# A graph network's edge phase: counts' product from behind the second product's first tile to the head of the step

## The chip, the cores and the metric

One core of one Trainium2 chip. The metric is the time of one execution on the device in microseconds (us). The kernel before took 1314.24 us, the median of three runs between 1310.16 and 1316.35.

## The reference, cut to what matters

Four graph layers with residual and layer norm, on 1250 nodes of 512 features and 21250 edges (sorted by their destination; each node has a loop). The change lies in the first layer, whose messages are worked out for each edge:

```
mish(x) = x * tanh(softplus(x))
h        = mish(concat(x[src], x[dst], edge_attr) @ W1 + b1)      # 21250 x 512
messages = mish(h @ W2 + b2)
agg      = segment_sum(messages, dst)
u        = mish(concat(x, agg) @ W3 + b3);  out = u @ W4 + b4
x        = layernorm(x + layernorm(x + out) * gamma + beta)
```

The other three layers need sums of x[src] over the edges into each node, and the numbers of such edges. The kernel gets them from one matrix of counts (how many edges lead from node n to node m), which it builds beside the messages, and multiplies by it in the later layers.

## The kernel before, in words

The kernel first makes two tables, P = x @ W1a + b1 and Q = x @ W1b, in DRAM (prepare). The edge phase then works on 42 blocks of 512 edges (NB = 42, four tiles of 128; the last block has fewer). Its five engine programs (edges_sync, edges_gpsimd, edges_vector, edges_scalar, edges_tensor) each run a step per block, from step -3 on, in an order that is written out by hand; steps 6 to 37 are a loop of two steps. In a step s the engines work on different blocks, and are tied by semaphores alone. Each engine takes its instructions in the written order, and a wait holds all that is behind it.

GpSimd gathers the rows of P and, added to them, of Q for the edges of a block (L228), and adds the block's window of counts (L681) and of message sums (L692) to DRAM. These go through its own queue. SyncE loads edge features.

TensorE in step s, before the change (L1066 to L1074):

- first(s+1, f) for four f, called the turns of rows below: four transposes of gathered rows (L1021), and two products with the edge features on top (L1026), to the four banks of ps_x1. The first of them waits for the gather and for VectorE's h1_of(s); the last lets ScalarE start its sigmoid for block s+1 (pre_ready).
- second(s, c) for four tiles c: h @ W2 as three products in parts, over four slices, so 12 matmuls of 512 columns (L1062). They go by turns to two banks, ps_x2[0] and ps_x2[1]. Tile 0 waits for lo_ready; tile c waits until the tile two before it is evacuated.
- adjacency(s), counts' product, between tile 0 and tile 1: a matmul of 427 columns in float16 for each tile of edges (L1035), of two one-hots, to its own bank ps_adj. It waits for the one-hots of block s (key_ready) and for the evacuation of block s-1's counts by ScalarE (adj_evac).
- sums(s-2), the window sums: eight matmuls (L1046) of one-hots with the messages' parts m_hi and m_lo, to ps_agg. They wait for the second half of message_low(s-2), among others.

VectorE in step s (L820 to L844): low(s) (L753), messages(s-2) (L771), message_high(s-2) (L780), the split of edge features for block s+3 (L736, L738), one-hots (count_one_hots L796, L797 for block s+1, one_hots L807 for s-1), x2_of(s,0) (L762, it evacuates tile 0), window_sums(s-3) (L818), more one-hots, message_low(s-2) half 0 (L787), x2_of(s,1), h1_of(s+1) in two halves (L746), x2_of(s,2), message_low(s-2) half 1 (L787), x2_of(s,3).

ScalarE in step s: sigmoid and arctangent of block s-1's second activation (L943, which waits for x2_of(s-1,3), and L948), sigmoid and arctangent of block s+1's first (L919, L924), the evacuation of counts (L912), sine of block s+1 in halves (L930), sine of s-1 (L953), and the high parts of h (L936). Two loads of an activation table lie between.

The last block has its own order, the drain: second(last,0), adjacency(last), second(last,1), sums and so on (L1087). After it come the node part of the first layer and three graph layers. Blocks that don't exist are left out, so that in step 0 there is no sums, and in step -1 only the turns of block 0.

Of the kernel before, what the change touches and what calls it, by code (L numbers as in the profile page):

```python
# [549 lines left out]
def edge_phase(nc, sb, pb, sem, edge_sem, sems_to_clear, ident, half_pi, relT, srcT, qT, idx_all, base_f, base_i, npass, iota_src,  # L550
# [11 lines left out]
    with ExitStack() as ctx:  # L562
# [446 lines left out]
        def edges_tensor(pe):  # L1009
            t = nc.tensor  # L1010

            def first(b, f):

                if b.real():
                    if f == 0:
                        pe.wait_ge(q_in[b.slot], b.slot_count(16 * TE))
                    if f % 2 == 0 and b.at(-1).real():
                        pe.wait_ge(h1_ready, b.at(-1).count(2, f // 2 + 1))
                    out = ps_x1[:, f * BE:(f + 1) * BE]
                    for c in range(TE):  # L1020
                        t.matmul(out[:, c * P:(c + 1) * P], G[:, b.slot, c * D + f * P:c * D + (f + 1) * P], ident[:, :],  # L1021
                                 start=(c == 0), stop=False, is_transpose=True)
                    if f == 0:
                        pe.wait_ge(ea_ready, b.count(1))
                    for i, w in enumerate((wc_hi, wc_lo)):
                        last = t.matmul(out, w[:, f * P:(f + 1) * P], ea_parts[:, b.slot, :], start=False, stop=(i == 1))  # L1026
                    last.then_inc(pre_ready, 1)

            def adjacency(b):
                if b.real():  # L1030
                    pe.wait_ge(key_ready, b.count(TE))
                    if b.at(-1).real():
                        pe.wait_ge(adj_evac, b.at(-1).count(1))
                    for k in range(b.tiles()):
                        last = t.matmul(ps_adj[:, 0:NC], oh_win[:, b.slot, k, :], oh_src[:, b.slot, k, :], start=(k == 0), stop=(k == b.tiles() - 1))  # L1035
                    last.then_inc(adj_ready, 1)

            def sums(b):
                if b.real():
                    pe.wait_ge(oh_ready, b.count(TE))  # L1040
                    pe.wait_ge(mlo_ready, b.count(2))
                    if b.at(-1).real():
                        pe.wait_ge(agg_evac, b.at(-1).count(1))
                    for k in range(b.tiles()):
                        for i, m in enumerate((m_hi, m_lo)):
                            last = t.matmul(ps_agg[:, :], oh_winr[:, b.slot, k, :], m[:, cols(k)], start=(k == 0 and i == 0),  # L1046
                                            stop=(k == b.tiles() - 1 and i == 1))
                    last.then_inc(agg_ready, 1)

            def second(b, c):  # L1050

                if b.real() and c < b.tiles():
                    if c == 0:
                        pe.wait_ge(lo_ready, b.count(2))
                    if c >= 2:
                        pe.wait_ge(x2_evac, b.count(TE, c - 1))
                    elif b.at(-1).real():
                        pe.wait_ge(x2_evac, b.at(-1).count(TE, c + 3))
                    for k in range(KD):
                        e = slice(k * BE + c * P, k * BE + (c + 1) * P)  # L1060
                        for i, (h, w) in enumerate(((hT_hi, w2_hi), (hT_hi, w2_lo), (hT_lo, w2_hi))):
                            last = t.matmul(ps_x2[c % 2][:, :], h[:, b.slot, e], w[:, k, :], start=(k == 0 and i == 0),  # L1062
                                            stop=(k == KD - 1 and i == 2))
                    last.then_inc(x2_ready, 1 if c + 1 < b.tiles() else TE - c)

            def step(s):  # L1066
                for f in range(KD):
                    first(s.at(1), f)
                second(s, 0)
                adjacency(s)  # L1070
                second(s, 1)
                second(s, 2)
                second(s, 3)
                sums(s.at(-2))  # L1074

            def one_pass(p):
                def node_part(r):
                    u, c0 = r // KD, r % KD * D
                    pe.wait_ge(xT_in[r], p * 32 + 32)
                    pe.sem_inc(turn, 1)  # L1080
                    for k in range(KD):
                        c = slice(c0 + k * P, c0 + (k + 1) * P)
                        for i, (h, w) in enumerate(((hT_hi, w3_hi), (hT_hi, w3_lo), (hT_lo, w3_hi))):
                            last_one = t.matmul(ps_z[r], h[:, u, c], w[:, k, :], start=(k == 0 and i == 0), stop=(k == KD - 1 and i == 2))
                    last_one.then_inc(zx_out, 1)

                def drain(last, b2nd, b3rd, b4th):  # L1087
                    second(last, 0)
                    adjacency(last)
                    second(last, 1)  # L1090
                    sums(b3rd)
                    second(last, 2)
                    second(last, 3)
                    pe.wait_ge(h1_ready, last.count(2))
                    node_part(0)
                    sums(b2nd)
                    node_part(1)
                    node_part(2)
                    sums(last)
                    pe.wait_ge(x2_evac, last.count(TE))  # L1100
                    pe.sem_inc(turn, 1)
                    for r in range(3, ZE):
                        node_part(r)
                steps(pe, p, step, drain)
# [977 lines left out]
```

## Time and profile before

| | |
|---|---|
| median of three runs | 1314.24 us |
| the profiled execution, its span | 1317.44 us, 1315.8 us |
| TensorE busy with matmuls | 1241.0 us, 94% |
| VectorE busy | 1020.1 us, 78% |
| ScalarE busy | 851.8 us, 65% |
| GpSimd busy | 697.9 us, 53% |
| L1062, second product, 2004 matmuls | 798.4 us busy |
| L1046 in 205 to 790 us, 266 matmuls | 105.0 us busy |
| L1035 in 205 to 790 us, 136 matmuls | 30.8 us busy |
| edge steps 0 to 40 | about 118 to 833 us |

Records of TensorE overlap, since matmuls are pipelined and their ends are modelled: a matmul of 512 columns has a record of 0.39 us, and the next one starts 0.23 us after it. So its busy time is not the sum of records, and the starts are what to compare. Weight loads (PEld) have records of their own. Idle time is given in brackets behind an instruction with what ended it; "issue" is time in which the engine waited for nothing that the profile shows.

### The profile page before, as it was taken

What the parts mean: (1) busy time and instruction counts of PE and PEld (TensorE: products, weight loads), DVE (VectorE), ACT (ScalarE), POOL (GpSimd) and SP (SyncE); (2) the same over time, 40 slices, a digit from 0 to 9 for tenths busy, and PEclk for the clock granted to TensorE, in tenths of its full rate; (3) what the DMA queues carried; (4) which work ended last, traced back from release to release, by engine and by line L of the source; (5) the groups of instructions that cost most, each with busy time, mean ns of one, the idle gap of its engine ahead of it and who ended that gap; (6) DMA issues with size and microseconds to landing.
All of it is one profiled execution on the core that took longest, in us unless ns stands there. A gap on an engine that the chain in (4) does not pass through costs nothing. (4 is left out here: it accounts for less than half of the span.)

```text
span 1315.8 us, 18959 instructions
## 1 busy us (share of the span) xinstructions
PE 1241.0 (94%) x5844; PEld 993.9 (76%) x5844; DVE 1020.1 (78%) x1799; ACT 851.8 (65%) x772; POOL 697.9 (53%) x482
## 2 busy tenths in 40 slices
PE   6976999999999999999999999978799987999998
PEld 5764777877777777877777777767587776888886
DVE  3425799999999999999999999866775247757444
ACT  2305999999999999999999999848523101212210
POOL 0036888888888888888888888342410000111000
PEclk9996999999999999999999999999899997999999
DMA  9996877777777777777787777798100620000001
GB/s 279 335 333 148 169 136 148 153 155 156 154 161 157 148 142 151 154 155 153 157 161 155 147 142 148 189 340 306 61 1 0 221 65 0 17 1 2 0 25 56
DMA packets 107195, 183.59 MB, mean 140 GB/s; under 512 B 34994, under 2 KB 44512, under 8 KB 106872
## 3 DMA queue, kind: packets, MB, share of 16 engines
q0 software_dynamic: 70704, 105.14, 41.0%
q1 hardware_dynamic: 29336, 65.40, 14.6%
q10 hardware_dynamic: 7088, 12.20, 2.9%
q8 instruction: 37, 0.61, 0.2%
q14 instruction: 30, 0.25, 0.1%
HBM read 141.21 MB, written 41.30 MB: 139 GB/s over the span
## 5 line engine op out<-in xcount | busy, mean ns | idle before, releaser
L228 POOL DMA_INDIRECT w_raw<-q_dram,idx_all x172 | 363.2, 2111 | 77.3 <-issue 61.5
L1062 PE MATMUL ps_x<-wA_hi,hT_hi 128*128 128x512 f32 x668 | 270.8, 405 | 1.3 <-DVE hT_lo L753 1.3
L1062 PE MATMUL ps_x<-wA_hi,hT_lo 128*128 128x512 f32 x668 | 264.0, 395 | 0.0
L1062 PE MATMUL ps_x<-wA_lo,hT_hi 128*128 128x512 f32 x668 | 263.6, 395 | 0.0
L228 POOL DMA_INDIRECT w_raw<-p_dram,idx_all x176 | 181.4, 1031 | 114.2 <-DMA q_dram<-x 60.9
L1062 PEld LDWEIGHTS ps_x<-wA_hi,hT_hi 128*128 128x128 f32 x668 | 125.4, 188 | 34.2 <-issue 1.9
L1062 PEld LDWEIGHTS ps_x<-wA_hi,hT_lo 128*128 128x128 f32 x668 | 125.2, 187 | 30.8
L1062 PEld LDWEIGHTS ps_x<-wA_lo,hT_hi 128*128 128x128 f32 x668 | 125.2, 187 | 28.5
L762 DVE TENSOR_TENSOR x<-ps_x,b 128x512 f32<-128x512 f32 x167 | 113.8, 682 | 27.0 <-PE ps_x L1062 25.1
L1743 POOL TENSOR_TENSOR tmp_n<-X,gam 128x512 f32<-128x512 f32 x10 | 13.9, 1395 | 227.0 <-DVE t_be L1828 182.4
L1021 PE MATMUL ps_x<-ident,w_raw 128*128 128x128 f32 x672 | 103.6, 278 | 19.0 <-issue 11.4
L1021 PEld LDWEIGHTS ps_x<-ident,w_raw 128*128 128x128 f32 x672 | 85.9, 144 | 43.7 <-issue 13.0
L746 DVE TENSOR_TENSOR h<-ps_x,h 128x1024 f32<-128x1024 f32 x84 | 98.3, 1210 | 3.7 <-ACT h L930 3.7
L787 DVE TENSOR_TENSOR m_lo<-m,m_hi 128x1024 fp32r<-128x1024 f32 x82 | 99.3, 1212 | 0.0
L753 DVE TENSOR_TENSOR hT_lo<-h,hT_hi 128x1024 fp32r<-128x1024 f32 x84 | 98.7, 1217 | 0.0
L771 DVE TENSOR_TENSOR m<-x,m 128x1024 f32<-128x1024 f32 x82 | 96.5, 1218 | 0.0
L930 ACT ACTIVATE h<-h,half_pi 128x1024 f32<-128x1024 f32 x84 | 92.1, 1144 | 0.5
L919 ACT ACTIVATE h<-ps_x 128x2048 f32<-128x2048 f32 x42 | 78.5, 1868 | 10.8 <-PE ps_x L1026 10.8
L936 ACT CAST hT_hi<-h 128x1024 fp32r<-128x1024 f32 x84 | 83.4, 1038 | 0.9 <-issue 0.5
L1977 PE MATMUL ps_sum<-U_hi,adjT_rest 128*128 128x512 f32 x210 | 82.6, 394 | 0.2 <-issue 0.2
L1026 PE MATMUL ps_x<-ea_parts,wc_hi 128*128 128x512 f32 x168 | 82.6, 491 | 0.0
L1977 PE MATMUL ps_sum<-U_lo,adjT_rest 128*128 128x512 f32 x210 | 81.9, 390 | 0.0
(268 smaller groups left out, 2853.6 us busy)
## 6 DMA issues: line engine op xcount, KB each, us to landing
ea_raw<-in_eaT SPq DMA_DIRECT2D x88, 128.0 KB
adj_dram<-adj_sb POOLq DMA_DIRECT2D x42, 210.2 KB
adj_dram<-agg_sb ACTq DMA_DIRECT2D x11, 640.5 KB, 12.0
U_lo<-adj_dram SPq DMA_DIRECT2D x10, 640.0 KB, 9.2
adjT_dram<-adjT_sb SPq DMA_DIRECT2D x10, 640.0 KB, 6.3
adjT_rest<-adjT_dram SPq DMA_DIRECT2D x7, 640.0 KB, 9.8
w_raw_g<-in_w SPq DMA_DIRECT2D x4, 1024.0 KB, 7.7
agg_dram<-agg_sb POOLq DMA_DIRECT2D x42, 84.0 KB
```

What stands on the lines that cost most here:

```text
L228: g.indirect_dma_start(G[:, slot, c * D:(c + 1) * D], None, rows, bass.IndirectOffsetOnAxis(ap=idx_all[:, i:i + 1], axis=0), **op).then_in ...
L746: v.tensor_tensor(h1[:, b.slot, c], ps_x1[:, c], h1[:, b.slot, c], ALU.mult).then_inc(h1_ready, 1)
L753: v.tensor_tensor(hT_lo[:, b.slot, c], h1[:, b.slot, c], hT_hi[:, b.slot, c].bitcast(F32), ALU.subtract).then_inc(lo_ready, 1)
L762: v.tensor_tensor(x2[:, b.slot, cols(c)], ps_x2[c % 2][:, :], b2[:, :], ALU.add).then_inc(x2_evac, 1 if c + 1 < b.tiles() else TE - c)
L771: v.tensor_tensor(m2[:, b.slot, c], x2[:, b.slot, c], m2[:, b.slot, c], ALU.mult).then_inc(m2_ready, 1)
L787: v.tensor_tensor(m_lo[:, c], m2[:, b.slot, c], m_hi[:, c].bitcast(F32), ALU.subtract).then_inc(mlo_ready, 1)
L930: a.activation(h1[:, b.slot, c], h1[:, b.slot, c], ACT.Sin, scale=-2.0, bias=half_pi[:, :]).then_inc(t1_ready, 1)
L936: a.copy(hT_hi[:, b.slot, c], h1[:, b.slot, c]).then_inc(hi_ready, 1)
L1021: t.matmul(out[:, c * P:(c + 1) * P], G[:, b.slot, c * D + f * P:c * D + (f + 1) * P], ident[:, :], start=(c == 0), stop=False, is_transpo ...
L1026: last = t.matmul(out, w[:, f * P:(f + 1) * P], ea_parts[:, b.slot, :], start=False, stop=(i == 1))
L1062: last = t.matmul(ps_x2[c % 2][:, :], h[:, b.slot, e], w[:, k, :], start=(k == 0 and i == 0), stop=(k == KD - 1 and i == 2))
L1977: last = t.matmul(ps_m[n % 2][:, :], adj_tile(r, k).bitcast(dt), u[:, cols(k)].bitcast(dt), start=(k == 0 and i == 0), stop=(k == R - 1 an ...
```

## The change

The call adjacency(s) moves from behind second(s, 0) to the head of TensorE's step, in front of the turns of rows. Its body and its waits are the same, and so are all other engines' programs and the drain.

```
             def step(s):
+                adjacency(s)
                 for f in range(KD):
                     first(s.at(1), f)
                 second(s, 0)
-                adjacency(s)
                 second(s, 1)
                 second(s, 2)
                 second(s, 3)
```

## Rows read from the trace of the kernel before

**Rows 1.** Windows: stretch, then busy us (instructions) of PE, PEld, DVE, ACT, POOL; clock, DMA.
```profile
205.00:800.00 595.00, 595.00 (x2873) 471.60 (x2872) 577.76 (x989) 560.99 (x409) 511.74 (x342) 1.00 0.77 153
```

**Rows 2.** Waits, 205 to 790: engine, line, for what; total us, times, longest.
```profile
ACT L943 <- DVE x L762: 28.9, 33, 1.2
DVE x L762 <- PE ps_x L1062: 14.5, 33, 0.5
...
PEld ps_agg L1046 <- issue: 4.8, 29, 0.2
```

**Rows 3.** Timeline of TensorE, 517 to 535: start, duration, what.
```profile
517.10 0.39 PE L1046 MATMUL ps_agg<-m_hi,oh_winr 128*128 128x512 f32 x1
...
522.58 0.40 PE L1062 MATMUL ps_x<-wA_hi,hT_hi 128*128 128x512 f32 x1
...
525.38 0.91 PE L1035 MATMUL ps_adj<-oh_src,oh_win 128*128 128x427 f16 x4
...
526.36 0.39 PE L1062 MATMUL ps_x<-wA_lo,hT_hi 128*128 128x512 f32 x1
...
534.52 0.39 PE L1046 MATMUL ps_agg<-m_hi,oh_winr 128*128 128x512 f32 x1
```

**Rows 4.** Timeline of VectorE, 508 to 527.
```profile
508.66 0.68 DVE L762 TENSOR_TENSOR x<-ps_x,b 128x512 f32<-128x512 f32 x1
...
509.86 0.32 DVE L796 TENSOR_SCALAR oh_src<-iota_src,srcT 128x427 f16<-128x427 f16 x1
...
512.79 2.35 DVE L746 TENSOR_TENSOR h<-ps_x,h 128x1024 f32<-128x1024 f32 x2
...
515.65 1.21 DVE L787 TENSOR_TENSOR m_lo<-m,m_hi 128x1024 fp32r<-128x1024 f32 x1
...
526.08 0.67 DVE L762 TENSOR_TENSOR x<-ps_x,b 128x512 f32<-128x512 f32 x1
```

**Rows 5.** Timeline of TensorE's weight loads, at the sums of that step.
```profile
516.99 0.19 PEld L1046 LDWEIGHTS ps_agg<-m_hi,oh_winr 128*128 128x128 f32 x1 [0.17 <-issue]
```

**Rows 6.** Timeline of VectorE and TensorE at the sums of step 2.
```profile
166.99 1.21 DVE L787 TENSOR_TENSOR m_lo<-m,m_hi 128x1024 fp32r<-128x1024 f32 x1
...
168.34 0.47 PE L1046 MATMUL ps_agg<-m_hi,oh_winr 128*128 128x512 f32 x1 [1.02 <-DVE m_lo L787]
...
168.65 0.39 PE L1046 MATMUL ps_agg<-m_lo,oh_winr 128*128 128x512 f32 x1
```

**Rows 7.** Timeline of TensorE and VectorE in step 39.
```profile
801.50 0.40 PE L1062 MATMUL ps_x<-wA_hi,hT_hi 128*128 128x512 f32 x1
...
804.51 0.69 DVE L762 TENSOR_TENSOR x<-ps_x,b 128x512 f32<-128x512 f32 x1 [0.41 <-PE ps_x L1062]
...
806.31 0.44 DVE L796 TENSOR_SCALAR oh_src<-iota_src,srcT 128x427 f16<-128x427 f16 x1
...
811.66 1.22 DVE L787 TENSOR_TENSOR m_lo<-m,m_hi 128x1024 fp32r<-128x1024 f32 x1
```

**Rows 8.** Timeline of ScalarE, 505 to 514.
```profile
505.73 1.86 ACT L919 ACTIVATE h<-ps_x 128x2048 f32<-128x2048 f32 x1
...
511.25 2.19 ACT L930 ACTIVATE h<-h,half_pi 128x1024 f32<-128x1024 f32 x2
```

**Rows 9.** Timeline of VectorE and TensorE, steps -1 to 0.
```profile
113.06 0.24 DVE L797 TENSOR_SCALAR oh_win<-iota_src,keyT 128x128 f16<-128x128 f16 x1
...
117.76 1.12 PE L1021 MATMUL ps_x<-ident,w_raw 128*128 128x128 f32 x4 [7.63 <-DVE h L746]
...
135.98 0.69 DVE L762 TENSOR_TENSOR x<-ps_x,b 128x512 f32<-128x512 f32 x1 [2.05 <-PE ps_x L1062]
```

**Rows 10.** Timeline of TensorE at the start of the drain.
```profile
834.16 0.49 PE L1062 MATMUL ps_x<-wA_hi,hT_hi 128*128 128x512 f32 x1 [1.26 <-DVE hT_lo L753]
```

**Rows 11.** Timeline of GpSimd, a gather of P rows in either step.
```profile
509.33 0.98 POOL L228 DMA_INDIRECT w_raw<-p_dram,idx_all  x1 [0.30 <-issue]
...
805.68 0.98 POOL L228 DMA_INDIRECT w_raw<-p_dram,idx_all  x1 [0.30 <-issue]
```

More of the change, by code:

```diff
@@ L1066, in step @@
             def step(s):
+                adjacency(s)
                 for f in range(KD):
@@ L1069, in step @@
                 second(s, 0)
-                adjacency(s)
                 second(s, 1)
```

## The prediction

> **What bounds the kernel now.** I read the windows first, to see where the time is: between 205 and 800 us, 45% of the span, TensorE has a product in flight all the time at a granted clock of 1.00, while VectorE is busy 578 of 595 us and ScalarE 561 [rows 1]. This is the middle of the edge phase, one step after another. Then the waits of that stretch, to see who waits for whom: in each of its 33 full steps VectorE waits 0.44 us for the second product's last tile (14.5 / 33) and ScalarE 0.88 us for VectorE (28.9 / 33); TensorE's matmuls wait for nobody, but the weight load that opens the window sums is late by a little, 4.8 us over 29 steps [rows 2]. The timeline of TensorE gives the step as it is now: sums from 517.10 and the turns of rows with the edge part behind them, the second product's tile 0 from 522.58, counts' product at 525.38, tiles 1 to 3, and sums again at 534.52 [rows 3]. That is 17.42 us, without a gap: 5.48 sums and turns, 2.80 tile 0, and 9.14 for counts and tiles 1 to 3.
>
> So TensorE bounds the step; the question is by how much, since the change adds no work. The VectorE timeline answers it. x2_of(s,0) starts at 508.66, and from there VectorE runs without a wait to the end of the second message_low, 515.65 + 1.21 = 516.86: 8.20 us [rows 4]. The sums wait for exactly this, and their weight load starts at 516.99, 0.13 after it, instead of with the product before as the others do (idle 0.17) [rows 5]. How long the hand-over takes at the least is seen in step 2, where TensorE really stood waiting (idle 1.02): message_low ends at 166.99 + 1.21 = 168.20, and the second product of the sums starts at 168.65, which with a spacing of 0.23 is as if the first had started at 168.42, 0.22 after [rows 6]. In the steady step it starts 517.10 - 516.86 = 0.24 after. **The slack at the sums is 0.02 us.** VectorE's other tie to TensorE in this stretch is the start of x2_of(s,0), which needs tile 0. In step 39, where VectorE did wait for it (idle 0.41), it starts 804.51 - 801.50 = 3.01 us after tile 0's first matmul [rows 7]. In the steady step this would allow 522.58 + 3.01 = 525.59, and VectorE comes at 526.08 [rows 3, 4]: slack 0.49. Together 0.51 us of slack in the cycle tile 0, x2_of(s,0), message_low, sums, turns, next tile 0.
>
> **The change, part by part.** It moves four matmuls and two waits, in the 41 steps 0 to 40; the last block's product, in the drain, stays. No DMA and no instruction of another engine moves.
>
> What the product costs TensorE: from 525.38 to the second product after it, 526.36, less that one's own spacing of 0.23, is 0.75 us; its records say the same, 0.91 less the 0.16 by which matmuls of 0.39 at a spacing of 0.23 overlap [rows 3]. In its new place it stands behind the sums and before the turns, a pair of neighbours that the trace does not have. The nearest row for a disturbed start is the opening of the sums in step 2, 0.31 to the next instead of 0.23 [rows 6]: 0.08 more, or as much less if a disturbance of that size around the product goes away. So 0.67 to 0.83, and I take 0.75, since four streams of the same length are the most of it in either place. TensorE's own step then stays at 17.42.
>
> The two waits at the head: VectorE writes block s+1's one-hots before h1_of, which starts at 512.79, and ScalarE evacuates the counts of block s before its sine at 511.25; the head of the next step, behind the sums, is at about 519 [rows 3, 4, 8]. Both are over by 6 us: nothing. If that cover were gone, TensorE would stand with the turns and all of the step behind it.
>
> What is later by it: tile 0 and all of the turns end 0.75 later with respect to the sums before them. The cycle without slack is now
> 8.20 (x2_of(s,0) to message_low) + 0.22 (hand-over) + 5.48 (sums, turns) + 0.75 (counts) + 3.01 (tile 0 to x2_of) = 17.66 us.
> Before, without the 0.75, it was 16.91, under TensorE's 17.42. It is now the longer of the two by 0.24 (0.16 to 0.32 by the bounds of the counts' cost). VectorE's 16.98 us of work (17.42 - 0.44) fit; its wait divides, some 0.45 before x2_of(s,0) and 0.2 before x2_of(s,3). TensorE stands 0.24 before each sums.
>
> ScalarE's first sigmoid starts at 505.73, when ScalarE comes free [rows 8]; the turns end at 522.58 less a step of 17.42, 505.16, and 0.21 after (3.01 less tile 0's 2.80) it could start. With the turns 0.75 later, and 0.24 for the stand at the sums, it waits some 0.6 for them. Its first sine half then ends 0.21 + (511.25 + 1.1 - 505.73) = 6.83 after the turns; VectorE needs that at 3.01 + (512.79 - 508.66) = 7.14: 0.3 to spare, hidden. ScalarE's idle 0.88 covers its wait. GpSimd's first gather of P rows waits for the turns, but it comes over 2 us after them: hidden; the queues get nothing new.
>
> The start: in step 0 TensorE stands 7.63 us until 117.76, and the product can go there, its last one-hot at 113.06 [rows 9]. Tiles 1 to 3 of step 0 end 0.75 earlier, and VectorE stood waiting for the last (2.05 before 135.98) [rows 9]; ScalarE's chain and then the sums of block 0, which wait for message_low, come about 0.7 earlier. From 0 (if it is ScalarE that holds step 1) to 1.5 (if step 1 gives it once more); I take 0.7.
>
> The sum: the sums of blocks 1 to 37 have 36 spacings between them, each 0.24 longer: 8.6; with the 0.7 off at the start +7.9 us. The drain begins with a wait of 1.26 of TensorE, for hT_lo [rows 10], but this follows the last tile through VectorE and is late with it, so nothing is given back. The program's later stages are as they were. From the profiled execution, 1317.4 us with 1.6 outside the span, 1325.3; that execution was 3.2 above the median of the runs, so for the median 1314.24 + 7.9 = **1322 us**.
>
> **Rivals.**
> *The cycle keeps its slack (not slower).* Place: the start of x2_of(s,0). It decides as soon as the product at the head costs under 0.51 us, or VectorE's stretch and the hand-over shrink by 0.24. Then the step is 17.42 as before and only the start's gain is left: 1314.2 - 0.7 = 1313.5, or 1312.7 with the larger start. For it: of the 0.24 at the sums 0.22 is one reading, in step 2. Against it: the records of the four, 0.91 less an overlap of 0.16, leave no room for 0.51, and VectorE's 8.20 has no idle time in it. A smaller miss, cycle at 17.5, gives 1316.
> *VectorE meets GpSimd.* The gathers of P rows run beside the one-hots. In the steady step a one-hot of 0.32 at 509.86 lies under the gather of 509.33 unharmed; in step 39, after the same kind of wait before x2_of(s,0), one at 806.31 near the end of the gather of 805.68 takes 0.44, and the stretch to message_low's end is 811.66 + 1.22 - 804.51 = 8.37 instead of 8.20 [rows 4, 7, 11]. In the changed step x2_of(s,0) comes after such a wait each time. If it costs 0.17 each time, the cycle is 17.83, 36 x 0.41 = 14.8, less 0.7: 1328. Against it: step 3, without the wait, also varies, and GpSimd's gathers will move with VectorE.
> Were one one-hot in each step held for the whole of a gather, 0.98 [rows 11], it would be 36 x 0.98 = 35 us, 1349; the 0.12 at 806.31 speaks against it, and it has 0.01 of this rival's chance.
> That strong form is a rule of the Trainium skill, SBUF — State Buffer, "Who interferes with whom": VectorE and GpSimd take a shared port pair as an exclusive lock, and the later one is blocked for the whole of the other's instruction. The trace agrees that they meet, not on the length.
> *The change does not reach the path*: TensorE held at the head by the one-hots or the evacuation. The 6 us above speak against it; its price, were the margin gone, has no bound but the step.
>
> **How the numbers follow.** The forecast, cycle of 17.58 to 17.74: 0.60, 1319 to 1325. Contention, to 1330: 0.15. Slack kept or nearly, 1313 to 1318: 0.20, of it 0.05 clearly faster by something in the start or in TensorE's neighbours that I don't see. Held at the head or other: 0.05. What can be told from no change here is 0.5%, 6.6 us, so 1320.8 and up is slower: four in five of the forecast's share, all of the contention's, 0.6 in all with a part of the others against the runs' own scatter of 6 us; same 0.34, faster 0.06. The range takes in the forecast, most of the contention and the kept slack: 1313 to 1329.
>
> **What would show it.** Right: steps of 17.6 to 17.7 us; a gap of about 0.24 before the first product of the sums, put down to m_lo; VectorE waiting before x2_of(s,0) and less before x2_of(s,3); ScalarE's L919 waiting 0.4 to 0.6 for the turns; the counts' product still 0.9 in its records. Wrong: steps of 17.42 with no gap, or one-hots above 0.32 and steps of 17.8 or more, or waits at the counts' product.

## The result, and the profile after

The changed kernel takes 1324.81 us (median of 8 runs, 1320.07 to 1327.42) against 1313.51 us before (8 runs, 1309.68 to 1316.35): ratio 1.0092, 95% interval 1.0073 to 1.0111. It is slower by 11 us; 1322 was forecast. The profiled execution took 1326.07 us, its span is 1324.4.

The windows of the changed kernel's middle stretch look as before, which is why they don't explain it [rows 1]:

```profile
205.00:800.00 595.00, 594.73 (x2819) 464.23 (x2819) 573.95 (x979) 558.11 (x405) 512.82 (x337) 1.00 0.76 152
```

The waits of 205 to 790 us name the places (engine, line, for what; total us, times, longest). ScalarE now waits 0.63 a step for the turns (21.4 / 34) and half as long for VectorE; the sums' weight load is later than it was, 0.43 instead of 0.17 [rows 2]. VectorE waits before x2_of twice a step:

```profile
ACT h L919 <- PE ps_x L1026: 21.4, 34, 0.9
PEld ps_agg L1046 <- issue: 14.1, 33, 0.7
ACT L943 <- DVE x L762: 12.9, 33, 0.5
...
DVE x L762 <- PE ps_x L1062: 8.8, 41, 0.3
DVE x L762 <- issue: 7.6, 23, 0.3
```

The timeline of TensorE in one step answers to [rows 3]. From the last product of tile 3 at 515.97 to the sums it is 0.39 us, where 0.23 is the spacing without a wait; from the first of the sums to the second it is 0.33. Counts' product takes 519.07 - 518.33 = 0.74, and the next sums come 534.05 - 516.36 = 17.69 after these:

```profile
515.97 0.40 PE L1062 MATMUL ps_x<-wA_hi,hT_lo 128*128 128x512 f32 x1
516.36 0.50 PE L1046 MATMUL ps_agg<-m_hi,oh_winr 128*128 128x512 f32 x1
516.69 0.40 PE L1046 MATMUL ps_agg<-m_lo,oh_winr 128*128 128x512 f32 x1
...
518.33 0.91 PE L1035 MATMUL ps_adj<-oh_src,oh_win 128*128 128x427 f16 x4
519.07 0.60 PE L1021 MATMUL ps_x<-ident,w_raw 128*128 128x128 f32 x4
...
522.70 0.40 PE L1062 MATMUL ps_x<-wA_hi,hT_hi 128*128 128x512 f32 x1
...
534.05 0.50 PE L1046 MATMUL ps_agg<-m_hi,oh_winr 128*128 128x512 f32 x1
```

The timeline of VectorE in the same step [rows 4]: it stands before x2_of(s,0), which comes 525.70 - 522.70 = 3.00 after tile 0's start, and the second message_low ends at 532.71 + 1.20 = 533.91, 8.21 later and 0.14 before the sums. The profile names no engine for the 0.33 in front of x2_of(s,0). That it is a wait for tile 0 is read from the starts: in all the loop's steps x2_of(s,0) comes 3.00 after tile 0, as in step 39 before, where the wait was put down to TensorE [rows 7].

```profile
525.70 0.69 DVE L762 TENSOR_TENSOR x<-ps_x,b 128x512 f32<-128x512 f32 x1 [0.33 <-issue]
...
532.71 1.20 DVE L787 TENSOR_TENSOR m_lo<-m,m_hi 128x1024 fp32r<-128x1024 f32 x1
534.10 0.69 DVE L762 TENSOR_TENSOR x<-ps_x,b 128x512 f32<-128x512 f32 x1 [0.18 <-PE ps_x L1062]
```

The cycle is closed: 6.34 (sums, counts, turns, from 516.36 to 522.70) + 3.00 + 8.21 + 0.14 = 17.69.

Landmarks on TensorE in all the profiles (us; "first" is the first turns of rows, "turns 1" those of step 0, "sums k" the first product of block k's sums, "node" the last product with W3 of the edge phase, "L1534" the first transposes of counts; the step is the loop column / 37):

```
kernel            first  ->turns 1  ->sums 0  ->sums 1  ->sums 38  step    ->node  ->L1534  ->end
before            103.30   14.46     50.58     17.51     645.03    17.433   35.57    2.11   447.24
before, again     100.87   14.29     50.63     17.51     645.79    17.454   35.60    2.28   446.93
changed           100.08   13.53     49.10     17.67     654.83    17.698   35.58    8.47   445.14
changed, second   102.26   13.97     49.59     17.65     655.93    17.728   35.59    4.39   444.82
changed, third     99.30   13.36     49.07     17.65     656.20    17.735   35.58    3.59   445.35
changed, fourth   100.38   14.05     49.58     17.66     656.04    17.731   35.57    2.63   443.79
e2 mid            101.65   14.35     50.55     17.72     656.37    17.740   35.59    2.26   445.71
e3 head+onehots   102.35   14.20     49.46     17.51     650.56    17.583   35.59    3.08   445.25
e4 before+onehots 101.23   14.29     50.58     17.51     647.51    17.500   35.58    1.98   445.82
e5 head+mlow      101.92   14.44     49.21     17.51     645.03    17.433   35.57    3.89   444.13
e6 before+mlow    101.16   14.70     50.10     17.51     644.78    17.426   35.59    2.37   445.19
e7 start only      98.40   14.04     48.95     17.66     645.82    17.455   35.58    2.68   446.47
e8 before, half   101.84   13.92     49.66     17.38     638.19    17.248   35.59    3.19   446.83
e9 head, half     102.03   13.70     49.18     17.29     642.55    17.366   35.58    2.72   444.05
```

The loss is in one column, the loop: 9.8 to 11.2 us between the profiles of the changed kernel and the first of before (9.0 to 10.4 against the second). A start shorter by 1.0 to 1.5 us, to the sums of block 0, stands against it. From the first turns to the node part the changed kernel takes 6.9 to 9.8 us more; the medians of the runs differ by 11.3. The first profile of the changed kernel has also 8.47 us in front of the first transposes of counts, and the experiments begin with whether that belongs to the change.

### The profile page after: what moved, and what is told of

Same layout as the page of the kernel before. It is cut to its first block and busy times, and to the rows that moved or that the text cites. A ratio compares the mean times of both kernels' runs of the same rounds, so it can differ in the third digit from the quotient of the medians.

```text
span 1324.4 us, 18959 instructions
## 1 busy us (share of the span) xinstructions
PE 1249.3 (94%) x5844; PEld 994.1 (75%) x5844; DVE 1024.0 (77%) x1799; ACT 855.9 (65%) x772; POOL 709.6 (54%) x482
## 5 line engine op out<-in xcount | busy, mean ns | idle before, releaser
L228 POOL DMA_INDIRECT w_raw<-q_dram,idx_all x172 | 321.6, 1870 | 76.2 <-issue 51.5
L228 POOL DMA_INDIRECT w_raw<-p_dram,idx_all x176 | 234.5, 1332 | 112.6 <-DMA q_dram<-x 59.3
L1062 PE MATMUL ps_x<-wA_hi,hT_hi 128*128 128x512 f32 x668 | 264.3, 396 | 1.3 <-DVE hT_lo L753 1.3
L762 DVE TENSOR_TENSOR x<-ps_x,b 128x512 f32<-128x512 f32 x167 | 114.2, 684 | 27.3 <-PE ps_x L1062 17.8
L919 ACT ACTIVATE h<-ps_x 128x2048 f32<-128x2048 f32 x42 | 79.2, 1887 | 32.3 <-PE ps_x L1026 32.3
```

The lines of the kernel that those rows point to most:

```text
L228: g.indirect_dma_start(G[:, slot, c * D:(c + 1) * D], None, rows, bass.IndirectOffsetOnAxis(ap=idx_all[:, i:i + 1], axis=0), **op).then_in ...
L762: v.tensor_tensor(x2[:, b.slot, cols(c)], ps_x2[c % 2][:, :], b2[:, :], ALU.add).then_inc(x2_evac, 1 if c + 1 < b.tiles() else TE - c)
```

## The experiments

"Before" is timed beside each call; ratios are against it.

**The changed kernel again.** No edit.

> The changed kernel once more, for its profile. The cycle theory (tile 0, x2_of(s,0), message_low, sums, counts, turns; 8.20 + 0.22 + 5.48 + 0.75 + 3.01): steps of 17.7 us with the sums 0.15 late in their starts. The tail theory (the rest of the loss lies behind the edge loop: GpSimd adds its counts 1.3 us after the sums' start instead of 3.4 before it, so its last additions land late and the loads of counts and sums for the first layer wait): again 8 us or so of idle time of TensorE before the first transposes of counts (L1534), against 1.7 in the kernel before. The rival for the tail, chance of one execution: 2 us there, and a span nearer 1320. Time: 1324 to 1326 by the first, 1320 to 1322 by the rival.

Measured: 1324.86 us (6 runs), ratio 1.0101 (1.0075 to 1.0128). Steps of 17.73 us, and the tail is short, 4.39, with GpSimd adding its counts 3.3 us before the sums' start. The rival for the tail holds: the 8 us was chance of one execution. But its time, 1320 to 1322, does not hold: the 4.1 us that the tail gives back are taken up by 2.2 more before the first turns, 0.9 more in the start and 1.1 more in the loop. Its steps go by turns, 17.69 and 17.8. Where they are 17.8, an instruction of VectorE behind x2_of(s,0) is held up beside a gather of GpSimd; where they are 17.69, the one that is held up stands in front of x2_of(s,0), where VectorE waits for tile 0 anyway. VectorE and then GpSimd in the step of 476 us (records of 0.48 and 0.39 for the usual 0.25 and 0.28; the gather runs from 478.00 to 478.99). The records overlap: from the start of the 0.48 to message_low it is 0.47 where 0.36 is usual, so the delay is 0.11:

```profile
478.27 0.33 DVE L796 TENSOR_SCALAR oh_src<-iota_src,srcT 128x427 f16<-128x427 f16 x1
478.51 0.48 DVE L797 TENSOR_SCALAR oh_win<-iota_src,keyT 128x128 f16<-128x128 f16 x1
478.68 0.39 DVE L807 TENSOR_SCALAR oh_winr<-iota_src,relT 128x128 fp32r<-128x128 f16 x1
478.98 1.21 DVE L787 TENSOR_TENSOR m_lo<-m,m_hi 128x1024 fp32r<-128x1024 f32 x1
```

```profile
478.00 0.99 POOL L228 DMA_INDIRECT w_raw<-p_dram,idx_all  x1 [0.30 <-DVE agg_sb L818]
```

**Counts' product between the turns and tile 0.**

```
             def step(s):
-                adjacency(s)
                 for f in range(KD):
                     first(s.at(1), f)
+                adjacency(s)
                 second(s, 0)
```

> Counts' product between the turns and tile 0, so neither at the head nor beside the sums; it is still in front of tile 0. The cycle theory: nothing changes against the changed kernel, steps of 17.7 us, ScalarE's L919 no longer waits for the turns by more than the sums' lateness, 1322 to 1326. The neighbour theory (the product costs more, or a wait bites, because it stands between the sums and the turns): steps of 17.43 as before, 1312 to 1315.

Measured: 1323.52 us, ratio 1.0085 (1.0066 to 1.0104), steps of 17.74. The product costs the same wherever it stands in front of tile 0; it is not its neighbours and not the head. ScalarE's L919 waits for the turns once in 205 to 790 us, instead of 0.63 in each step, and the step is the same, so ScalarE's wait isn't what lengthens it. Only the start differs: 50.55 to the sums of block 0, as before, where the head has 49.1 to 49.6.

**The head, with the second half of the one-hots in front of x2_of(s,0).**

```
+                count_one_hots(s.at(1), 2)
+                one_hots(s.at(-1), 2)
+                count_one_hots(s.at(1), 3)
+                one_hots(s.at(-1), 3)
                 x2_of(s, 0)
                 window_sums(s.at(-3))
-                count_one_hots(s.at(1), 2)
-                one_hots(s.at(-1), 2)
-                count_one_hots(s.at(1), 3)
-                one_hots(s.at(-1), 3)
```

> The changed kernel with VectorE's second two pairs of one-hots (1.2 us) moved from behind x2_of(s,0) to in front of it; VectorE's work is the same. The cycle theory: the stretch from x2_of(s,0) to message_low is 7.0 instead of 8.2, the cycle 16.5 and no longer the longest, so steps of 17.43 (TensorE's own) and 9 to 10 us less in the edge loop: 1312 to 1316, or 3 to 5 us more if the tail stays late. The neighbour theory: steps of 17.7 as now, 1324. A third, VectorE meeting GpSimd: steps somewhere between, with one-hots above 0.32.

Measured: 1319.09 us (12 runs), ratio 1.0049 (1.0034 to 1.0064), steps of 17.58. That falls between, and the forecast of 17.43 was wrong. The timelines of VectorE, ScalarE and TensorE in this kernel:

```profile
482.60 0.69 DVE L762 TENSOR_TENSOR x<-ps_x,b 128x512 f32<-128x512 f32 x1 [0.30 <-PE ps_x L1062]
...
492.72 0.68 DVE L762 TENSOR_TENSOR x<-ps_x,b 128x512 f32<-128x512 f32 x1
...
495.05 0.68 DVE L762 TENSOR_TENSOR x<-ps_x,b 128x512 f32<-128x512 f32 x1
495.79 1.23 DVE L746 TENSOR_TENSOR h<-ps_x,h 128x1024 f32<-128x1024 f32 x1
...
498.66 1.22 DVE L787 TENSOR_TENSOR m_lo<-m,m_hi 128x1024 fp32r<-128x1024 f32 x1
500.18 0.69 DVE L762 TENSOR_TENSOR x<-ps_x,b 128x512 f32<-128x512 f32 x1 [0.30 <-PE ps_x L1062]
```

```profile
489.05 1.89 ACT L919 ACTIVATE h<-ps_x 128x2048 f32<-128x2048 f32 x1 [0.50 <-PE ps_x L1026]
...
494.61 1.15 ACT L930 ACTIVATE h<-h,half_pi 128x1024 f32<-128x1024 f32 x1
```

```profile
482.44 0.49 PE L1046 MATMUL ps_agg<-m_hi,oh_winr 128*128 128x512 f32 x1
...
488.77 0.40 PE L1062 MATMUL ps_x<-wA_hi,hT_hi 128*128 128x512 f32 x1
...
500.01 0.49 PE L1046 MATMUL ps_agg<-m_hi,oh_winr 128*128 128x512 f32 x1
```

x2_of(s,0) no longer waits, so the first cycle is broken. The next longest goes through ScalarE. From the sums at 482.44 to tile 0, which is where the turns end, it is 6.33 (the product at the head is in it); 0.28 later ScalarE's first sigmoid starts, which stood waiting for the turns; its chain to the end of the first half of the sine, at 494.61 + 1.15 = 495.76, takes 6.71; VectorE's h1_of starts 0.03 after, at 495.79, though x2_of(s,1) in front of it began 0.74 earlier and 0.60 is usual; message_low ends 4.09 later, at 499.88, and the sums start 0.13 after that. 6.33 + 0.28 + 6.71 + 0.03 + 4.09 + 0.13 = 17.57. In 31 of 32 steps of the loop h1_of starts 0.03 to 0.06 after the sine, and in none of the changed kernel's steps (0.16 to 0.46). There this cycle is 17.55, only 0.14 below the one through x2_of(s,0), and shortening that one alone could not bring the step below it.

The expectations that follow were written with another reading of this run: a cycle over two steps, with 17.28 for VectorE from x2_of(s,3) at 482.60 to message_low's end. It gives 17.57 too, but the 17.28 has VectorE's wait for the sine in it, 0.14 in this step. VectorE's own part is 17.14 here and 17.23 on average over the loop, since some one-hots are slower than in the kernel before, which makes that cycle 17.50 here and 17.55 on average. The two are close, and the one through ScalarE is the longer. This is read from the trace; no run tests it by itself.

**The kernel before, with the same one-hots in front.**

> The kernel before with the same move of one-hots on VectorE. The cycle theory: TensorE's 17.43 was the longest and stays so: steps of 17.43, no change, 1311 to 1316; the weight load of the sums is no longer late. The rival, that GpSimd's phase against VectorE sets the tail: the loop as before but idle time before L1534 moved by 3 us or more either way.

Measured: 1314.52 us, ratio 1.0020 (1.0005 to 1.0035), steps of 17.50 (by turns 17.45 and 17.54) where 17.43 was expected. The product is in its old place, no h1_of waits for a sine here, and the cycle over two steps explains it: sums, a whole step of TensorE to the end of the next tile 3 (17.43), 0.20 to x2_of(s,3), VectorE to the end of message_low, 0.23 to the sums. VectorE's part is 491.45 - 481.33 = 10.12 and 498.46 - 491.45 = 7.01, together 17.13 instead of 16.99 (8.79 + 8.20) in the kernel before, and (17.43 + 0.20 + 17.13 + 0.23) / 2 = 17.50. VectorE's idle 0.31 before x2_of(s,3) is part of that cycle and no slack. What lengthens VectorE is when the one-hots run: L796 takes 373 ns on average there, 340 in the kernel before. The tail stayed at 2.

```profile
481.33 0.69 DVE L762 TENSOR_TENSOR x<-ps_x,b 128x512 f32<-128x512 f32 x1 [0.31 <-PE ps_x L1062]
...
491.45 0.68 DVE L762 TENSOR_TENSOR x<-ps_x,b 128x512 f32<-128x512 f32 x1
...
497.25 1.21 DVE L787 TENSOR_TENSOR m_lo<-m,m_hi 128x1024 fp32r<-128x1024 f32 x1
```

**The head, with the second message_low in front of x2_of(s,2).** This leaves the one-hots where they are.

```
                 h1_of(s.at(1), 0)
                 h1_of(s.at(1), 1)
-                x2_of(s, 2)
                 message_low(s.at(-2), 1)
+                x2_of(s, 2)
                 x2_of(s, 3)
```

> The changed kernel with VectorE's second message_low (1.2 us) in front of x2_of(s,2) instead of behind it. VectorE's work and the place of its one-hots are as they are. Two cycles are now held responsible. First, tile 0, x2_of(s,0), message_low, sums, counts, turns: the stretch falls from 8.2 to 7.6, the cycle from 17.69 to 17.1. Second, found in the kernel with moved one-hots, a cycle over two steps: TensorE's step from the sums to the end of tile 3 (17.43), 0.20, VectorE from x2_of(s,3) to the next message_low (17.0 in the changed kernel, 17.28 there, which gave (17.43 + 0.20 + 17.28 + 0.23) / 2 = 17.57 and was measured as 17.58); it falls by 0.3. So steps of 17.43, 10 us less than the changed kernel in the loop, no lateness of the sums, and with the start's gain of 1.0 to 1.5 about 1 us under the kernel before: 1310 to 1314. The rival, that the head's place costs by itself or that GpSimd's contention sets the step: 17.6 or more, 1318 and up.

Measured: 1312.67 us (12 runs), ratio 0.9993 (0.9978 to 1.0007), steps of 17.433. The whole loss is gone with one line moved on another engine, and the product still at the head. The move takes 0.6 out of the cycle through x2_of(s,0) and out of the one through ScalarE, and 0.3 out of VectorE's part of the one over two steps. All are then under TensorE's 17.43. Timeline of VectorE and of TensorE: x2_of(s,0) still waits for tile 0, but message_low ends at 512.52 + 1.21 = 513.73, 0.59 before the sums, which follow tile 3 at 0.24:

```profile
506.12 0.69 DVE L762 TENSOR_TENSOR x<-ps_x,b 128x512 f32<-128x512 f32 x1 [0.17 <-issue]
...
512.52 1.21 DVE L787 TENSOR_TENSOR m_lo<-m,m_hi 128x1024 fp32r<-128x1024 f32 x1
```

```profile
514.08 0.39 PE L1062 MATMUL ps_x<-wA_hi,hT_lo 128*128 128x512 f32 x1
514.32 0.39 PE L1046 MATMUL ps_agg<-m_hi,oh_winr 128*128 128x512 f32 x1
```

**The kernel before with the same move.**

> The kernel before with the same move of message_low. If TensorE's 17.43 alone set its step, nothing changes: 17.43 us a step, 1310 to 1315; only the weight load of the sums comes with the product before, 0.23 ahead. If the kernel before was held by a cycle through VectorE and TensorE's step is really shorter, the step falls below 17.43 and the time by up to 10 us.

Measured: 1310.87 us (12 runs), ratio 0.9981 (0.9965 to 0.9996), steps of 17.426. TensorE's own step is 17.43 and no shorter. This is the best of the versions that make all counts. Of its 2.7 us under its neighbour the loop accounts for 0.3 to 1.0; the rest I can't place.

**The head in the start only.**

```
             def step(s):
+                head = s.it2 is None and s.k < LOOP_FROM
+                if head:
+                    adjacency(s)
...
                 second(s, 0)
-                adjacency(s)
+                if not head:
+                    adjacency(s)
```

> Counts' product at the head in the steps up to 5 only, and in the old place from step 6 on. The start theory (the product fills TensorE's wait in step 0 and ScalarE's chain starts earlier): from the first product of step 0's turns to the sums of block 0 49.1 to 49.6 us instead of 50.6, then steps 2 to 5 of 17.7 and all others 17.43: 0 to 1 us under the kernel before, 1310 to 1314. The rival, that the place in the start sets GpSimd's phase and by it something of the loop or the tail: steps of the loop other than 17.43, or over 4 us idle before L1534.

Measured: 1315.19 us, ratio 1.0020 (1.0003 to 1.0037); the profiled execution has a span of 1309.6. The columns are as the start theory has them: 48.95 to the sums of block 0 instead of 50.6, and given back are 0.15 at the next and 0.8 in the loop, where some steps are still at the head. The time does not show the gain; the median is even 1.6 above. Time before the first turns alone varies by 5 us between profiles (98.4 to 103.3), and the profiled execution is the lowest of the twelve (1311.29 to 1323.12), so its parts don't account for the median. A gain in time from the start is not shown, and why the median lies above its neighbour stays open.

**The kernel before with half of counts' product** (the counts of the last two tiles of edges of each block are left out).

```
-                    for k in range(b.tiles()):
-                        last = t.matmul(ps_adj[:, 0:NC], ..., start=(k == 0), stop=(k == b.tiles() - 1))
+                    for k in range(2):
+                        last = t.matmul(ps_adj[:, 0:NC], ..., start=(k == 0), stop=(k == 1))
```

> The kernel before with counts' product over the first two tiles of edges of a block only (the counts of the others are left out); VectorE still makes all one-hots. TensorE's own step becomes 17.43 - 0.37 = 17.06. If that alone bounded the kernel before: steps of 17.06, 14 us less, 1298. By the two-step cycle, (17.06 + 0.20 + 16.99 + 0.23) / 2 = 17.24: steps of 17.24, 7 us less, 1305, with the sums late by 0.2. If VectorE alone bounded it, 16.99 and 1296.

Measured: 1308.40 us (8 runs), ratio 0.9959 (0.9943 to 0.9975), steps of 17.248: the two-step cycle's 17.24, not TensorE's 17.06. The loop is 6.8 us shorter, about the 7 that were expected; the time is 5.2 under the neighbour's and 3.4 above the 1305 expected. Of the 0.37 taken from the engine that was busy all the time half came back. In the middle of the loop the steps go by turns, 17.32 and 17.17, as a cycle over two steps may. TensorE's sums and VectorE between two of them:

```profile
476.30 0.50 PE L1046 MATMUL ps_agg<-m_hi,oh_winr 128*128 128x512 f32 x1
...
493.62 0.50 PE L1046 MATMUL ps_agg<-m_hi,oh_winr 128*128 128x512 f32 x1
...
510.80 0.49 PE L1046 MATMUL ps_agg<-m_hi,oh_winr 128*128 128x512 f32 x1
```

```profile
493.68 0.69 DVE L762 TENSOR_TENSOR x<-ps_x,b 128x512 f32<-128x512 f32 x1 [0.20 <-PE ps_x L1062]
...
502.47 0.68 DVE L762 TENSOR_TENSOR x<-ps_x,b 128x512 f32<-128x512 f32 x1
...
509.46 1.21 DVE L787 TENSOR_TENSOR m_lo<-m,m_hi 128x1024 fp32r<-128x1024 f32 x1
```

From the sums at 476.30 to x2_of(s,3) at 493.68 is a step of TensorE, with what the wait at the sums adds to it, and the hand-over, 17.38; VectorE then needs 16.99, to 510.67, without a wait; the sums start 0.13 after, at 510.80. Together 34.50, twice 17.25.

**The head with half of counts' product** (the same counts left out; the same edit on the changed kernel).

> The changed kernel with counts' product over the first two tiles of edges only (the counts of the others are left out). The cycle through tile 0 has the product in it, so it falls by 0.37 from 17.70 (17.73 with its contention) to 17.33 or 17.36; TensorE's own step is 17.06 and the two-step cycle 17.24, both shorter. So steps of 17.33 to 17.36, 0.1 above the same cut in the old place (17.25), and 1309 to 1312. If the head's place cost a fixed 0.26 over whatever else bounds the step, it would be 17.5; if the two cycles were a story, 17.06.

Measured: 1311.42 us (12 runs), ratio 0.9985 (0.9967 to 1.0002), steps of 17.366. With the full product the head is at 17.698 to 17.735: the step falls by 0.33 to 0.37, nearly all of the 0.37 taken from the product, while at the old place the same cut brought 0.19.

**The changed kernel a third and a fourth time, and the kernel before again**, one execution each.

> The changed kernel a third time, for the phase of GpSimd and the tail. The phase theory: where GpSimd adds its counts 1.3 us after the sums' start, as in the first profile, the first transposes of counts wait 8 us and the part behind the edge phase's last product takes 453 to 454 us; where it adds them 3.3 before, as in the second profile, 2 to 5 us and 448 to 450. The rival: tail and phase vary without each other.

> As the third: phase of 1.3 after the sums with a long tail, or of 3.3 before with a short one. Either way the step in the loop is 17.68 to 17.74.

> The kernel before once more, for the scatter of its parts: steps of 17.43, GpSimd 3.4 before the sums, and 447 to 450 us behind the edge phase's last product. Its time before the first turns varies by some us (98 to 103 so far), and this is where executions of one kernel differ.

Measured: 1321.78 and 1321.38 us for the changed kernel, 1315.55 for the kernel before. Both of the changed kernel have GpSimd 3.3 before the sums, 3.6 and 2.6 us before L1534, and 448.9 and 446.4 us behind the node part; the kernel before has 449.2 and 449.35. Its second profile has steps of 17.454 on average because three late ones are 17.59, 17.83 and 17.54; in the longest, instructions of VectorE take up to 0.2 longer beside gathers. So the long tail came once in four, together with the late phase, in the profile whose GpSimd adds its counts 1.3 us after the sums' start. That the one causes the other was argued and not tested. The loss in the loop does not depend on it: it is there in all four.

## Why the prediction was right, and where it was off

The mechanism was the forecast's: the cycle through x2_of(s,0) became longer than TensorE's own step. Point by point:

- *What bounds the step, and by how little.* TensorE's 17.42, slack 0.02 at the sums and 0.49 at x2_of(s,0). Right for the cycle that the change lengthens: with it the sums stand, an earlier message_low takes all of the loss away (e5), and a product shorter by 0.37 shortens the step by nearly as much (e9).
- *The cycle of 17.66.* Measured 17.69 in the first profile and 17.73 in the three others. Its terms: counts 0.74 (0.75 forecast); VectorE's stretch 8.21 in the step shown (8.20), in the others 8.2 and 8.3 by turns; tile 0 to x2_of 3.00 (3.01); hand-over 0.22 forecast, measured as 0.14 to the sums' start and 0.10 more to their second product, 0.24. The steps are 0.04 to 0.07 over the forecast: 0.01 is the hand-over and the rest is VectorE's stretch. In the first profile it is 0.02 longer in most steps, and two steps are 17.96 and 17.98, with a one-hot of 0.6 beside a gather in each; in the others it is the second rival, instructions held up behind x2_of(s,0), at about a third of its price.
- *The place in the step.* That the head as such costs nothing, and its waits neither, is shown by e2.
- *ScalarE.* It waits 0.63 for the turns (0.6 forecast), and VectorE's h1_of still waits for no sine. But 0.3 to spare was twice too much: the first sigmoid starts 0.28 after the turns and not 0.21, its sine half ends 6.69 after that and not 6.62, and h1_of needs another 0.03. At the median it starts 0.17 after the sine, so 0.14 were left. The change doesn't hang on it; the experiment with the one-hots did (e3).
- *The start.* 0.7 forecast. To the sums of block 0 the head takes 1.0 to 1.5 us less, and 0.2 to 1.1 less already to the turns of step 0. With the product in front of tile 0 but behind the turns (e2) it is 50.55 as before, so the gain comes from the product filling TensorE's wait; the size was taken too small.
- *The count of steps.* 36 spacings were counted; 37 were longer, those from the sums of block 1 to those of block 38 (the last by 0.1), and the one in front of them by 0.15. This and the step's size make the loop 9.8 to 11.2 against 8.6.
- *The sum.* Two terms were too small, the loop by 0.4 to 2.6 us and the start's gain, with the part up to the turns of step 0, by 0.6 to 1.8, and they go against each other: of the 7.9 forecast the profiles show 6.9 to 9.8 in the edge phase. That this is so close is in part luck. The median moved by 11.3, and the rest of that no profile places: the parts before the first turns and behind the edge phase vary by as much between executions of one kernel.
- *The drain* gives nothing back: 35.57 us from the sums of block 38 to the node part before, 35.58 after.

One thing the forecast did not see, though its number did not hang on it: it read VectorE's idle 0.44 before x2_of(s,3) as free. The kernel before stood at the meeting of two bounds, TensorE's 17.43 and a cycle over two steps, (17.43 + 0.20 + 16.99 + 0.23) / 2 = 17.43. e4 and e8 went as this cycle says; in e3 the cycle through ScalarE was a little longer.

One rival was priced wrong in its own terms: a one-hot held for the whole of a gather would make the cycle 17.66 + 0.98 = 18.64 and the time 1357; the 1349 leave out the 0.24. No step of the changed kernel comes near it, 17.98 being the longest.

The profiled executions differ by 8.6 us in span and the medians by 11.3. The part before the first turns was 3.2 shorter in the changed kernel's profile and the tail 4.3 longer; the other three profiles of the changed kernel don't repeat the long tail, and the part in front varies in both kernels.

## What to carry to other kernels

When an engine is busy all the time, the slack to look for is not its own but that of the cycles that pass through it: add up one such cycle, from an instruction back to itself in the next step (and in the one after), with the hand-overs, and compare it with the step. Work moved ahead of a product that another engine waits for lengthens that cycle even though no engine gets more work. Look at the second longest cycle as well, for it decides how much shortening the first can bring, and let no hidden wait into a cycle's sum: a stretch in which an engine stood, if only for 0.1 us, belongs to another cycle. And the cure can be on the other engine: what the busy engine waits for goes ahead of what nobody waits for yet.

## What the runs showed of the hardware

- A matmul that had to wait at a semaphore starts 0.13 to 0.14 us after VectorE's record ends, and its successor 0.33 instead of 0.23 after it: a short stand costs 0.10 more than the gap in front of it shows.
- Four float16 products of 427 columns take TensorE 0.74 to 0.75 us whether they stand between float32 products or between those and transposes.
- The same one-hot has a record of 0.25 us or 0.48 by where it falls beside a gather of GpSimd, and what follows it is 0.11 late. In the kernel before, none of the 204 one-hots of 205 to 790 us that lie wholly inside a gather is longer than usual; the 34 that are longer, by 0.06 to 0.08 us, all run over a gather's end. With half of the one-hots moved in front of x2_of(s,0), VectorE needs 0.14 us more a step (e4), and 0.24 on average in e3, its wait for the sine left out.
- VectorE's h1_of starts 0.03 us after the end of the sine on ScalarE that it waited for (e3).
- Four executions of one kernel kept GpSimd in one of two phases against TensorE, 3.3 us before the sums or 1.3 us after, each for the whole loop.
